# A reordered seam, a cut-up compression and a new last step in the cross-attention of a one-core transformer layer

## The reference

```python
C_q = Q @ Wq_d                       # Q = layernorm(x); 64 latent features
C_kv = K @ Wkv_d                     # K = context; 1601 rows x 32 latent features
CqWqk = (C_q @ W_qk).reshape(b, n, H, LKV)          # H = 16, LKV = 32
scores = jnp.einsum('bnhl,bkl->bhnk', CqWqk, C_kv) / jnp.sqrt(LKV)
attn = jax.nn.softmax(scores, axis=-1)
V_up = (C_kv @ Wv_u).reshape(b, nkv, H, HD)
out = jnp.einsum('bhnk,bkhd->bnhd', attn, V_up)
```

## Time and profile before

| | us |
|---|---|
| median of 3 runs | 900.59 |
| profiled execution | 901.27 |
| its span, first to last instruction | 899.2 |
| TensorE busy in the span | 855.6 (95%) |
| VectorE, ScalarE, GpSimd busy | 606.5, 522.6, 459.1 |
| cross-attention ends about | 285.1 |

### The profile page before, as it was taken

How to read it: one execution, slowest core, us unless ns; L and a number is a source line. 1 busy time by engine, 2 the same in 40 slices (tenths; PEclk the granted TensorE clock), 3 DMA queues, 4 the chain that set the end, 5 groups by cost and what they waited for, 6 DMA issues and landing times.

```text
span 899.2 us, 15523 instructions
## 1 busy us (share of the span) xinstructions
PE 855.6 (95%) x5338; PEld 652.4 (73%) x5338; DVE 606.5 (67%) x993; ACT 522.6 (58%) x1013; POOL 459.1 (51%) x294
## 2 busy tenths in 40 slices
PE   6899999999997979999999999999999999899998
PEld 4455555554543768888888888888888887788886
DVE  4865576557634358768587685876858769777784
ACT  4755556555654457567575675756757577555552
POOL 2589887887652044544545445454454545144430
PEclk9979999999988999999999999999999999999999
DMA  9544444104302525014050240501405004446521
GB/s 366 186 172 159 155 166 169 34 10 114 94 1 89 193 82 212 24 59 176 0 210 23 63 170 0 210 23 63 171 0 210 12 1 136 146 141 208 184 99 47
DMA packets 42338, 102.96 MB, mean 115 GB/s; under 512 B 7858, under 2 KB 12978, under 8 KB 41394
## 3 DMA queue, kind: packets, MB, share of 16 engines
q1 hardware_dynamic: 42002, 102.06, 32.8%
q10 hardware_dynamic: 288, 0.26, 0.1%
HBM read 96.95 MB, written 1.05 MB: 109 GB/s over the span
## 4 chain that ended last, share of the span: by engine, by line
PE 60%; DVE 2%; POOL 1%; DMA 1%; ACT 1%; issue 0%; SPq 0%; POOLq 0%; DVEq 0%
PE psum L1408 11%; PE psum L1389 10%; PE psum L1524 9%; PE psum L1462 8%; PE psum L1420 6%; PE psum L1538 4%; PE psum L1447 3%; PE psum L1438 3%; PE psum L1443 3%; PE psum L1429 1%; PE psum L1441 1%; PE psum L1439 1%; DMA ffn_raw<-in_L_ffn_mean_w_dram 1%; POOL head_probs L1901 0%; POOL ffn_quant L1921 0%; POOL ffn_raw L1921 0%
## 5 line engine op out<-in xcount | busy, mean ns | idle before, releaser
L1901 POOL TENSOR_TENSOR head_probs<-head_probs,inverse_den 128x576 f32<-128x576 f32 x128 | 147.2, 1151 | 201.5 <-DVE inverse_den L1756 201.5
L1010 DVE TENSOR_REDUCE max_part<-psum 128x1 f32<-128x804 f32 x128 | 121.1, 991 | 41.5 <-PE psum L698 41.1
L905 ACT ACTIVATE probs<-psum 128x512 f32<-128x512 f32 (+1 forms) x208 | 106.4, 610 | 54.1 <-PE psum L720 53.4
L1638 ACT ACTIVATE head_probs<-psum,neg_max 128x576 f32<-128x576 f32 x128 | 94.6, 739 | 50.2 <-DVE neg_max L1773 49.7
L1773 DVE TENSOR_REDUCE neg_max<-psum 128x1 f32<-128x576 f32 x128 | 96.9, 757 | 21.9 <-PE psum L1408 20.5
L567 POOL TENSOR_TENSOR prob_sums<-prob_sums,probs 128x1024 f32<-128x1024 f32 (+1 forms) x42 | 100.1, 2384 | 16.6 <-ACT probs L905 12.0
L1408 PE MATMUL psum<-k_high,query_t_high 128*128 (+1 forms) x256 | 86.1, 336 | 1.9 <-DVE query_t_low L1728 1.4
L720 PE MATMUL psum<-q_t,c_t 97*128 97x512 f32 (+1 forms) x208 | 78.0, 449 | 8.4 <-ACT probs L905 5.7
L1749 DVE TENSOR_TENSOR probs_t_low<-psum,probs_t_high 128x512 fp32r<-128x512 f32 x124 | 84.8, 684 | 1.0
L567 POOL TENSOR_TENSOR prob_sums<-probs 128x1024 f32<-128x1024 f32 x30 | 71.2, 2377 | 25.8 <-ACT probs L905 25.7
L1921 POOL TENSOR_TENSOR ffn_quant<-ffn_raw 128x1536 f32<-128x1536 f32 x13 | 45.6, 3511 | 67.7 <-DVE ffn_w_low L1835 26.9
(11 more groups left out here) (227 smaller groups left out, 1927.1 us busy)
## 6 DMA issues: line engine op xcount, KB each, us to landing
ctx_t_odd<-in_ctx_dram SPq DMA_DIRECT2D x4, 3202.0 KB, 11.3
ffn_raw<-in_L_ffn_w_dram SPq DMA_DIRECT2D x42, 256.0 KB, 3.8
ffn_raw<-in_L_ffn_mean_w_dram SPq DMA_DIRECT2D x42, 256.0 KB, 4.1
w_piece<-in_L_ffn_w_dram SPq DMA_DIRECT2D x21, 512.0 KB, 6.5
w_piece<-in_L_ffn_mean_w_dram SPq DMA_DIRECT2D x21, 512.0 KB, 7.6
cache<-in_ctx_dram SPq DMA_DIRECT2D x3, 3202.0 KB, 11.7
wq_nat<-in_L_attn_wq_dram SPq DMA_DIRECT2D x32, 256.0 KB, 7.3
wo_nat<-in_L_attn_wo_dram SPq DMA_DIRECT2D x32, 256.0 KB, 3.4
```

The source lines that it names most:

```text
L905: act.activation(prob_buffer(b, t)[0:rows, half * BANK:(half + 1) * BANK], psum[0:rows, n % SCORE_BANKS, :], ACT.Exp, scale=XSCALE).then_i ...
L1010: dve.tensor_reduce(max_part[:, qt, pair:pair + 1], psum[:, bank:bank + 2, 0:PIECE_KEYS], AX.XY, ALU.max).then_inc(s_max, 1)
L1638: act.activation(probs[:, qt, :].rearrange("p (a k) -> p a k", a=2), psum[:, 2 * (qt % 2):2 * (qt % 2) + 2, 0:HALF], ACT.Exp, bias=neg_max ...
L1901: pool.tensor_tensor(probs[:, qt, :], probs[:, qt, :], rden[:, qt:qt + 1].to_broadcast([P, KEYS]), ALU.mult).then_inc(s["norm"], 1)
```

## The change

- Steps 0 to 4: `tail_and_denominators` is cut in two. `tail_and_first` (tail and the first group, four matmuls) stands behind compress, ahead of turn_max; `other_denominators` (four more) stands behind the two score tiles that are computed ahead. The first maximum of the following step is issued between these two tiles, and VectorE takes it at that place.
- `copy_den`: ScalarE copies one half, VectorE the other, behind that first maximum. `compressed_high` moves behind the first four exponentials of the next step and behind copy_den; `compressed_low` moves behind GpSimd's first add. VectorE does copy_u ahead of place_values.
- Steps 5 and 6: shift_row comes ahead of copy_den on ScalarE.
- Step 0: compress(2) goes to bank 3 and is cut into pieces between the first scores; rope_matrix moves behind step 6. compress(3) and later go to bank 5.
- Step 7 has its own list, `last_step`: values in units of two tiles, denominators in rounds among the scores, tile 11 and 12 straight from the probabilities.

```diff
-COMPRESS_BANK = (4, 3, 6) + (4,) * (BATCH - 3)
+COMPRESS_BANK = (4, 3, 3) + (5,) * (BATCH - 3)
...
+                    if t == 1 and b + 2 < BATCH:
+                        compressed_low(b + 2)
...
+            def last_step(b):
+
+                scores(b, 2)
+                scores(b, 3)
+                values(b, range(0, 1))
+                scores(b, 4)
+                mix(b - 1)
+                scores(b, 5)
+                values(b, range(1, 2))
+                for u in range(2, UNITS - 2):
+                    scores(b, 2 * u + 2)
+                    scores(b, 2 * u + 3)
+                    values(b, range(u, u + 1))
+                    if u == 3:
+                        pe.wait_ge(s_d, 2 * b)
+                        denominator_round(b, (0, 1), True)
+                scores(b, KT - 1)
+                values(b, range(UNITS - 2, UNITS - 1))
+                denominator_round(b, (2, 3), False)
+                last_tail(b)
...
+            def tail_and_first(b):
+
+                pe.wait_ge(s_max, MAXIMA * (b + 2) - 1)
                 pe.wait_ge(s_exp, HALVES * (b + 1))
-                pe.wait_ge(s_add, adds_through(b, parts[0][-1]))
+                pe.wait_ge(s_add, adds_through(b, GROUPED[b][0][-1]))
...
+            def other_denominators(b):
+
+                for n in range(1, len(GROUPED[b]), 2):
+                    pe.wait_ge(s_add, adds_through(b, GROUPED[b][n + 1][-1]))
...
+            compress(2, (0,))
             scores(0, 0)
+            compress(2, (1,))
             scores(0, 1)
+            compress(2, (2,))
+            max_scores(1, 0)
...
                 if b + 3 < BATCH:
                     compress(b + 3)
-                    turn_max(b + 1)
+                tail_and_first(b)
+                if b + 3 >= BATCH:
+                    other_denominators(b)
+                turn_max(b + 1)
+                if b + 3 < BATCH:
                     natural(b + 3)
-                else:
-                    tail_and_denominators(b)
-                    if lead:
-                        turn_max(b + 1)
-                if lead:
-                    scores(b + 1, 0)
-                    scores(b + 1, 1)
+                scores(b + 1, 0)
+                if b + 2 < BATCH:
+                    max_scores(b + 2, 0)
+                scores(b + 1, 1)
                 if b + 3 < BATCH:
-                    tail_and_denominators(b)
+                    other_denominators(b)
+            last_step(BATCH - 1)
             mix(BATCH - 1)
...
-                for half in range(2):
-                    act.activation(u_all[2 * LKV:P, half, :],
-                                   psum[half * 2 * LKV:(half + 1) * 2 * LKV, DEN_BANK, :],
-                                   ACT.Copy).then_inc(s_d, 1)
+                act.activation(u_all[2 * LKV:P, 0, :], psum[0:2 * LKV, DEN_BANK, :], ACT.Copy).then_inc(s_d, 1)
...
-                    if t == 1 and 0 < b < BATCH - 2:
-                        copy_den(b - 1)
+                    if t == 1 and b > 0:
+                        if b < BATCH - 2:
+                            copy_den(b - 1)
+                        if b + 2 < BATCH:
+                            compressed_high(b + 2)
...
+            def copy_den(b):
+                dve.wait_ge(s_den, b + 1)
+                wait(dve, s_o, b)
+                dve.tensor_copy(u_all[2 * LKV:P, 1, :], psum[2 * LKV:P, DEN_BANK, :]).then_inc(s_d, 1)
...
-            rope_matrix()
+            take_max(1, 0)
...
+                copy_u(b)
                 if b + 3 < BATCH:
                     place_values(b + 3)
-                copy_u(b)
+                if b + 2 < BATCH:
+                    take_max(b + 2, 0)
+                copy_den(b)
+                if b + 2 == BATCH:
+                    rope_matrix()
```

More of the change, by code:

```diff
@@ L721, in scores, with denominator_round @@
                               rhs[:, half * BANK:(half + 1) * BANK], start=True, stop=True).then_inc(s_sb, 1)
+            def denominator_round(b, sources, first):
+                for n in sources:
+                    wait(pe, s_add, adds_through(b, GROUPED[b][n][-1]))
+                for half in range(2):
+                    for odd, n in enumerate(sources):
+                        at = 2 * LKV * half + LKV * odd
+                        pe.matmul(psum[at:at + LKV, DEN_BANK, :], ones[:, :],
+                                  sum_buffer(b, n)[:, half * BANK:(half + 1) * BANK], start=first, stop=False)
@@ new lines, in last_tail @@
+            def last_tail(b):
+                pe.wait_ge(s_exp, HALVES * (b + 1))
+                for half in range(2):
+                    at, cols = 2 * LKV * half, slice(half * BANK, (half + 1) * BANK)
+                    mm = pe.matmul(psum[at:at + LKV, U_BANK, :], c_nat[0:TAIL, b % 3, KT - 1, :],
+                                   prob_buffer(b, KT - 1)[0:TAIL, cols], start=False, stop=True)
+                    pe.matmul(psum[at + LKV:at + 2 * LKV, DEN_BANK, :], ones[:, :], prob_buffer(b, KT - 2)[:, cols],
+                              start=False, stop=False)
+                mm.then_inc(s_pv, 1)
+                pe.wait_ge(s_add, adds_before(b + 1))
+                for half in range(2):
+                    at, cols = 2 * LKV * half, slice(half * BANK, (half + 1) * BANK)
+                    pe.matmul(psum[at:at + LKV, DEN_BANK, :], ones[0:TAIL, :], prob_buffer(b, KT - 1)[0:TAIL, cols],
+                              start=False, stop=True)
+                    mm = pe.matmul(psum[at + LKV:at + 2 * LKV, DEN_BANK, :], ones[:, :], sum_buffer(b, 4)[:, cols],
+                                   start=False, stop=True)
+                mm.then_inc(s_den, 1)
@@ L841, in _ @@
             pe.wait_ge(s_wv, 32)
+            compress(2, (0,))
             scores(0, 0)
+            compress(2, (1,))
             scores(0, 1)
-            for b in range(BATCH):
-                lead = b + 1 < BATCH
+            compress(2, (2,))
+            max_scores(1, 0)
+            for b in range(BATCH - 1):
                 def maximum(i):
-                    if lead:
-                        max_scores(b + 1, i)
-                maximum(0)
+                    max_scores(b + 1, i)
+                if b == 0:
+                    compress(2, (3, DC))
                 scores(b, 2)
```

47 lines of the change are left out of this document (16 added, 31 removed).

## The result

| | median us | mean granted clock of its runs | ratio to the kernel before |
|---|---|---|---|
| before (23 runs of the last comparison) | 900.46 | .984 | |
| after, 16 runs | 897.21 (890.24 to 900.86) | .984 | 0.9949 [0.9929, 0.9968] |
| after, 12 runs | 898.26 | .981 | 0.9964 [0.9938, 0.9991] |
| after, 12 runs | 898.83 | .981 | 0.9968 [0.9946, 0.9991] |
| after, 12 runs | 895.64 | .984 | 0.9949 [0.9924, 0.9974] |

The change makes the kernel 0.3 to 0.5% faster, about 4 us. A gain of 9.15 us and a time of 891.5 were forecast; the first median, 897.21, lies outside the range (886.0 to 896.5), and the gain is under half of the forecast. The profiled execution of the changed kernel took 890.24 us (span 887.8), which is nearly the forecast. That nearness is partly luck: this execution gained 11.0 us on the profiled one of before, 8.3 in the stage that was changed and 3.1 behind it.

What follows compares the result with a forecast made beforehand. TensorE, busy 855.6 of 899.2 us, was taken as the bound. Gains 3.3 - 0.1 + 1.75 + 0.3 + 3.9 = 9.15 us, off the 900.59 median, gave 891.5 us; range 886.0 to 896.5.

Steps and rivals of the forecast that it cites:

- the sentence on the clock: Cross-attention stage: low clock of 7.9 us in the first step, 6.9 in the last, none in a steady step.
- four rivals: Small gain (895 us), large gain (886), slower (905), and the early maximum holding up scores by 0.3 us a seam.
- the small gain: Seams give 0 for 1.75 us, last step 2.2 for 3.9: 5.7 us gained, 895, or 898; chance 0.25.
- ScalarE's row of work: At the seams, copy, high part and exponentials in a row lose what the holes give: 0 for 1.75 us.
- the first step's clock: Small-gain case where the first step's clock does not return early either: 2.5 us left, 898; small gain's chance 0.25.
- a last step that stays low for longer: Small-gain cause: low clock in the last step lasts twice as long, gaining 2.2 us for 3.9.
- First step: Compress(2) cut between scores, rope_matrix moved: fourth maximum at 54.2 for 57.54, gain 3.3 us, less 0.1 for GpSimd.
- Seams: Between steps, five seams: eighth score goes out 0.35 us earlier at each, 1.75 us in all.
- Step 5: Seam behind step 5: shift row first, one denominator copy goes to VectorE, gain 0.3 us.
- Last step: New list and split copies: final mix 5.4 us earlier at full clock, less 1.5 for low clock: gain 3.9 us.
- The slower rival: Keys of step b+3 placed 2.7 us late at each of five seams: 905 us; slower or nothing 0.06.

Runs made afterwards that it cites:

- the ends alone: Changed kernel with the five seams in the order of before; new first step, last step and copies behind steps 5 to 7 kept: 896.64 us, 0.9955.
- the second profile: Profiled execution from a repeat of the changed kernel, no edit: span 896.1 us; that repeat's median was 898.26 us.
- new seams with the old list: Changed kernel with the last step's list in the order of before, copies still split: 900.04 us in 11 runs, 0.9985.
- the wider hole: Kernel before with an extra ScalarE copy of 0.6 us ahead of its denominator copies at five seams: 908.41 us, 1.0074.

## Why the prediction was wrong

**The step that failed** is the sentence on the clock, "none in a steady step". It was read off one profiled execution of the kernel before and carried over to a kernel whose seams I had just rearranged. I had worked out that a hole of about 1.2 us would stay ahead of the eighth score (0.91 came), and charged it only as waiting. What the runs showed in its place: steady steps of 31.35, 31.30, 29.92 and 29.87 us with a granted clock of 0.89 and 0.94 in two of four profiled executions of the changed kernel. In all its runs the mean clock is .9825, for .9835 before (too small a difference to tell from chance), although the ends alone raise it to .9874. As an estimate, at some 0.55 us for each .001 (the slope over the runs: 577 us per unit after, 522 before), the .0049 between the ends alone and the whole change are 2.7 us: about what the five seams give at full clock, 2.3. The early maximum alone is of that size: putting it back raised the clock by .0060 beside the changed kernel, 3.3 us at that slope, and 3.6 were measured. None of the four rivals named a fall in a steady step. The medians, 895.64 to 898.83, lie between the two figures of the small gain (895 and 898), but that is luck: of its causes, ScalarE's row of work did not happen (ScalarE was on time to 0.15 us) and the first step's clock did return. Only its third, a last step that stays low for longer, came in part: two of the four profiles have 0.82 over 32.6 us there, 3.6 us, where the sum charged 1.5.

The Trainium skill (TensorE: Matmul & The Clock Gate, A second HAM failure mode: psum-queue depth-cycling) describes a kernel whose short idle times between groups of matmuls make the clock swing. I had weighed that page only for the first step. This case agrees in part: the clock fell behind holes of 0.91 and 1.18 us in steps where TensorE is otherwise busy 28.1 to 28.4 us, but with 0.90 us and more work beside the hole it mostly did not.

Point by point, by the terms of the sum, against the profiled execution:

- First step: 3.3 less 0.1 forecast, 2.54 measured in the profile at .994, from the turn to the fourth maximum, which starts at 54.84 for 57.54 (54.2 was worked out). The clock came back at the second chunk, as worked out: the score pair at 47.52 takes 0.73 where that at 45.46 took 1.22. Mechanism right, somewhat too large.

```profile
45.46 1.22 PE L719 MATMUL psum<-q_t,c_t 97*128 97x512 f32 x2
46.61 0.98 PE L649 MATMUL psum<-cache,wkv_d 128*32 128x384 f32 x8
47.52 0.73 PE L719 MATMUL psum<-q_t,c_t 97*128 97x512 f32 x2
...
54.84 0.63 PE L697 MATMUL psum<-c_t,q_t 96*128 96x402 f32 x2
```

- Seams: 1.75 forecast, 2.3 at full clock. Right in size, but attributed partly to the wrong edit: the early maximum was to fill the hole ahead of the fourth score, and with it put back the step is as short. And at full clock only: in the second profile two of the four steady steps lose 2.4 us again.
- Step 5: 0.3 forecast, about 0.2.
- Last step: 3.9 forecast as 5.4 at full clock less 1.5 for the clock. Measured in the first profile are 3.18 with the clock at 1.00 all through. So both parts were off, and partly cancel, which is luck: the full-clock work was put 2.2 us too short (final mix 22.06 us behind the turn worked out, 24.26 measured). What I left out shows in each unit of four scores and four value matmuls (x8 in the row), where a score waits for the exponential of the one before:

```profile
261.42 0.95 PE L719 MATMUL psum<-q_t,c_t 97*128 97x512 f32 x3
261.95 2.06 ACT L955 ACTIVATE probs<-psum 128x512 f32<-128x512 f32 x4 [0.54 <-PE psum L719]
262.60 0.49 PE L719 MATMUL psum<-q_t,c_t 97*128 97x512 f32 x1 [0.23 <-ACT probs L955]
263.03 1.06 PE L785 MATMUL psum<-probs,c_nat 128*32 128x512 f32 x8
```

Such a unit lasts 2.60 us (260.43 to 263.03), where 4 x 0.23 + 0.93 = 1.85 was counted. There are three of them, 2.2 us too long together when the denominator round in the third is taken off, and I had 1.2 for all such waits. So the gain of this edit is mostly the clock that it keeps, not the shorter tail: in this stretch the clock fell in all four profiles with the old list (before twice, new seams with the old list, the wider hole), and in four of twelve with the new one. Few profiles, each of one execution, and two kernels with other seams among them: a sign, not a proof.
- The slower rival did not come: the keys were placed in time, and no row shows TensorE waiting for them.

What stays open: why one execution of the same instructions keeps the clock at the seams and another loses it. Two profiled executions of the changed kernel that lost it did so in the same steps (both have 0.89 in the step behind the second mix, 31.35 and 31.30 us, and 0.82 from the sixth mix to the seventh), which does not look like noise from moment to moment; what sets the course was not found.

## What to carry to other kernels

Where TensorE is over 90% busy and a step mixes wide matmuls with a block of narrow ones, read the granted clock of every step in several executions before you price a change, and price what gathers or adds idle time as clock as well as waiting. One profile shows one such course of the clock; the mean clock of many runs, compared between kernels that are measured side by side, is the number that tells. A reorder that wins 0.5 us of a step can be worth nothing, and spare matmuls in idle time that cannot be avoided are worth a try.

## What the runs showed of the hardware

- A single core, with TensorE busy 28.1 of 29.4 us, can be granted 1.2 GHz for part of such a step: two of four profiled executions of the changed kernel show it. The step then costs 1.9 us more (31.35 for 29.42), and the one from the sixth mix to the seventh 3.6 (32.58 for 28.94).
- Added matmuls whose result nobody reads cost no time that these runs can show: 893.82 us with 15 of them in the holes, against 895.6 to 898.8 for the changed kernel in other comparisons; 889.49 with five in the last step against 892.63; 896.23 with 15 outside a hole, 3.3 us of work, against 895.64. Each of these differences is within the uncertainty. The mean clock is .989 with 15 of them at either place, against .981 to .984 without.
- Order alone, with the same instructions and the same length of a step at full clock (29.38 and 29.41), moved the mean clock of the runs from .9895 to .9835 in one comparison.
